# Attention on one core: the products with v in one burst of nine key tiles a unit instead of three bursts of three, with 18 buffers of probabilities instead of 9

## The reference, cut to what matters

```python
scores = jnp.einsum('bhqd,bhkd->bhqk', q, k) / math.sqrt(HEAD_DIM)
masked = jnp.where(causal[None, None], scores, NEG)
chunk_max = padded.reshape(b, N_HEADS, s, n_chunks, CHUNK).max(axis=-1)
_, topk_idx = jax.lax.top_k(chunk_max, k_top)
...
final = jnp.where(allowed, scores, NEG)
attn = jax.nn.softmax(final, axis=-1)
out = jnp.einsum('bhqk,bhkd->bhqd', attn, v)
```

## Time and profile before

| | |
|---|---|
| time, median of 3 runs | 1484.44 us (1482.44 to 1486.02) |
| profiled execution: its time | 1490.9 us |
| profiled execution: its span | 1489.0 us |
| PE busy over the span | 1292.4 us (87%) |
| DVE busy | 1021.5 us (69%) |
| ACT busy | 873.5 us (59%) |
| L1305, exponents (ACT) | 576 of 612 ns |
| L1225, masked scores (PE) | 576 of 396 ns |
| L1244, products with v (PE) | 4608 records of 276 ns |

### The profile page before, as it was taken

The page is one execution under the profiler, slowest core; times in us unless marked ns, Lnnn a source line. Parts: engine busy times, 40 slices in busy tenths (PEclk is TensorE's granted clock), DMA queues, the critical chain, the costliest instruction groups (busy, mean ns, idle before and its releaser), DMA issues. The chain is left out here.

```text
span 1489.0 us, 34856 instructions
## 1 busy us (share of the span) xinstructions
PE 1292.4 (87%) x10654; PEld 706.9 (47%) x10750; DVE 1021.5 (69%) x3215; ACT 873.5 (59%) x1605; POOL 449.2 (30%) x1388
## 2 busy tenths in 40 slices
PE   8957999999996996699899898998988989986995
PEld 3423444444443553355455455554555545543653
DVE  5875656556563599588788787887878878852563
ACT  2524625444250565377787687786767867872553
POOL 3530000000002233233334333433434334331665
PEclk9975999999998998599999999999999999998997
DMA  9310000000000266301110011110111101002221
GB/s 325 158 43 0 1 1 0 0 0 0 0 1 3 71 164 164 131 26 40 41 39 32 11 39 41 39 39 8 36 41 39 39 7 39 9 9 57 57 79 43
DMA packets 65131, 69.73 MB, mean 47 GB/s; under 512 B 35214, under 2 KB 53774, under 8 KB 64300
## 3 DMA queue, kind: packets, MB, share of 16 engines
q1 hardware_dynamic: 64940, 67.38, 14.2%
HBM read 36.96 MB, written 19.92 MB: 38 GB/s over the span
## 5 line engine op out<-in xcount | busy, mean ns | idle before, releaser
L1305 ACT ACTIVATE arena<-bank 128x512 f32<-128x512 f32 x576 | 340.2, 612 | 171.4 <-PE bank L1225 97.8
L1365 DVE TENSOR_REDUCE arena<-bank 128x32 f32<-128x512 f32 x528 | 343.8, 683 | 104.3 <-PE bank L1211 65.7
L1211 PE MATMUL bank<-arena 96*128 96x512 bf16 (+3 forms) x832 | 235.7, 333 | 25.2 <-issue 20.6
L1225 PE MATMUL bank<-arena 123*128 123x512 bf16 x576 | 222.8, 396 | 14.9 <-ACT arena L1305 12.3
L1244 PE MATMUL bank<-arena 128*32 128x128 f32 x4608 | 176.3, 276 | 12.6 <-ACT arena L1305 12.4
L579 PE MATMUL bank<-arena 128*128 128x512 f16 (+1 forms) x704 | 173.3, 390 | 0.0
L1475 POOL TENSOR_SCALAR arena<-arena 128x128 bf16<-128x128 bf16 x384 | 142.6, 371 | 47.5 <-DVE arena L1425 25.5
L1244 PEld LDWEIGHTS bank<-arena 128*32 128x32 f32 x4608 | 124.8, 109 | 43.2 <-ACT arena L1305 23.8
L1463 POOL TENSOR_TENSOR arena<-arena 128x4 f32<-128x4 f32 x128 | 25.4, 199 | 373.0 <-DVEq L1400 343.1
L205 POOL TENSOR_TENSOR arena<-arena 128x1 f32<-128x1 f32 x32 | 7.5, 234 | 388.8 <-DVE arena L201 388.4
L591 PE MATMUL bank<-arena 128*128 128x512 f16 (+1 forms) x528 | 118.4, 386 | 3.1 <-ACT arena L651 3.1
(11 more groups left out here) (183 smaller groups left out, 2252.6 us busy)
## 6 DMA issues: line engine op xcount, KB each, us to landing
arena<-qk_rows SPq DMA_DIRECT2D x16, 960.0 KB, 4.8
qk_rows<-arena SPq DMA_DIRECT2D x16, 768.0 KB, 4.1
arena<-arena SPq DMA_DIRECT2D x32, 256.0 KB, 2.9
arena<-in_x SPq DMA_DIRECT2D x4, 1024.0 KB, 12.4
out<-arena SPq DMA_DIRECT2D x16, 256.0 KB, 2.1
qk_rows<-arena SPq DMA_DIRECT2D x16, 192.0 KB, 4.6
arena<-in_down_qT SPq DMA_DIRECT2D x1, 2816.0 KB, 25.6
arena<-in_up_qT SPq DMA_DIRECT2D x1, 2752.0 KB, 19.4
```

The source lines that it names most:

```text
L1211: last = pe.matmul(bank[:, at:at + k1 - k0], query_aug[st.slot][0:ROWS, h * P:(h + 1) * P], key_aug[st.p][0:ROWS, k0:k1], start=True, stop ...
L1225: last = pe.matmul(bank[:, :], key_aug[st.p][0:KROWS, j * P:(j + 1) * P], query_aug[st.slot][0:KROWS, f * N:(f + 1) * N], start=True, stop ...
L1305: act.activation(probs[u % PROBS], back_bank[u % 2][:, :], ACT.Exp, scale=float(HD) ** -0.5).then_inc(probs_ready, 1)
L1365: dve.tensor_reduce(out=cm[:, number * per:(number + 1) * per], in_=score_bank[bank_of_score(front, number)][:, :].rearrange("p (c d) -> p ...
```

## The change

All tiles of a unit are weighed in one burst. With `BURST = 9` the schedule has one step "burst" a unit, at 0.985; the two at 0.448 and 0.733 are gone. The number of matmuls is the same. There are 18 buffers of probabilities, the nine new ones from the space that other small tiles of the stage are taken from. The exponent's wait on `summed` now points 18 tiles back instead of 9. ACT, DVE and POOL have the same work in the same order.

```diff
-    BURST, PROBS = 3, 9
+    EARLY_PROBS = 9
+    BURST, PROBS = 9, 18
...
-    probs = [take(N) for _ in range(PROBS)]
+    probs = [(take if n < EARLY_PROBS else spare)(N) for n in range(PROBS)]
```

## The result

The changed kernel takes 1507.03 us (median of 4 runs, 1505.23 to 1510.89), the kernel before 1485.23 beside it: a ratio of 1.0152, 95% interval 1.0126 to 1.0178, or 19 to 26 us more. The forecast was 1513 and 1497 to 1533. The profiled execution spans 1504.9 us. That is only 15.9 more than the one before, because what stands ahead of the first exponent took 7.0 us less in it (and what follows the last one 2.1 more); from the first exponent to the last, attention takes 736.2 us instead of 715.4, 20.8 more.

A forecast was written before the change was run, and what follows sets the result against it. A loop through ACT and PE bounds attention, no engine being full. Four units pay 5.28 us and get back 3.50, so 1.78 more; 16 times that, 28.5 us, gives 1513 us, range 1497 to 1533.

The forecast's parts named there:

- The loop through both engines: Attention units: first masked tile, nine exponents, last burst, next first masked tile set the time; chance 0.79 for 1497 to 1533.
- the 96.5 us: Attention: claimed as all the time ACT waits for masked tiles.
- Paid, 0.22 us a tile: Burst behind a unit's last exponent: six tiles more cost 1.32 us a unit, 5.28 us in four.
- Given back, kind by kind: Second halves of the four unit kinds: last exponent comes earlier by 0.88, 0.71, 0.85 and 1.06, together 3.50 us.
- Counted at nothing: DVE's wait for scores, copies of the sums behind the burst, and the new buffers: claimed to add nothing.
- sixteen times that: All of attention: 1.78 us more in four units, taken 16 times, gives 28.5 us, all units counted alike.
- for scores that arrive late: Upper side of the range: 20 us allowed above the forecast, up to 1533.
- the bound of 15 us: Second halves of units: if every idle moment of ACT there went, the change would still cost 15 us.
- PE is the bound: Rival, PE's bursts: each has a fixed 0.22 us, 128 go, 28 us faster, near 1456; chance 0.10.
- Nothing comes back: Rival, second halves: freed time lost as scores wait for DVE, 1569, half lost 1541; chance 0.07 for more than 1533.

The follow-up runs named there:

- e3: Kernel before with 18 buffers and two bursts a unit, three tiles at 0.448 and six at the end: 1482.18 us, ratio 0.9972 to before.
- e2: Kernel before with 18 buffers and two bursts a unit, six tiles at 0.733 and three at the end: 1517.72 us, ratio 1.0215 to before.
- e4: Changed kernel with its one end burst weighing only three of a unit's nine tiles, the rest left out: 1423.95 us, ratio 0.9582 to before.
- e1: Kernel before with only the 18 buffers added, still three bursts of three a unit: 1485.78 us, ratio 1.0007 to before.
- v3: Kernel before with 18 buffers, each unit's third burst of three and the copies of the sums moved into the next unit: 1441.54 us, ratio 0.9705.
- v9: Changed kernel with its burst of nine moved into the next unit at 0.11, copies of the sums behind it: 1477.79 us, ratio 0.9945 to before.

## Why the prediction was right

- *The bound.* The loop through both engines was the right reading: e3, before, after and e2, with 2, 3, 1 and 2 bursts a unit, fall in the order that the loop forecast (1484, 1485, 1513, 1521; measured changes of -4, 0, 22 and 32 us), not in that of the number of bursts, and two of them are told apart by 36 us with the same number. One row was misread on the way: the 96.5 us are not "in all" what ACT waits for masked tiles, which is 166.8; nothing in the sum uses it.
- *Paid, 0.22 us a tile.* The burst of 72 records holds PE for 2.11 us (1062.85 to 1064.96) against 0.80: 1.31, forecast 1.32. e4 has the term alone: 5.08 for four units, forecast 5.28.
- *Given back, kind by kind.* The units 7+0, 4+3, 6+1 and 5+2 grew by 0.60, 0.43, 0.47 and 0.24 us (11.57, 11.33, 11.00 and 11.08 against 10.97, 10.90, 10.53 and 10.84). Forecast were 1.32 less 0.71, 0.88, 0.85 and 1.06, which is 0.61, 0.44, 0.47 and 0.26. In 4+3 the last masked tile starts 1.44 behind the seventh exponent (1061.57 - 1060.13), before 2.33 (1056.12 - 1053.79): 0.89 earlier, forecast 0.88.
- *Counted at nothing.* First halves unchanged, DVE's busy time unchanged, and e1 shows the buffers at nothing. DVE does wait longer for scores, 130.3 us in attention instead of 108.5, but the idle time that it had took this up: the units grew by no more than the terms of the sum.
- *The size of the whole.* Forecast were 28.5 us, measured 22 (19 to 26). The term that was off is "sixteen times that". The units agree; what the sum did not have is what lies between them. PE jumps back six times in attention's loop over the groups, with a wait each time (20.6 us in all before, 18.8 after). In the profiled executions the units at these six places were 29.6 us longer than their kind before and 24.7 after (28.6 in e1, 26.5 in e2). The waits are 1.8 of these 4.9 us; the rest goes with PE's granted clock behind them. These are the 6 us from PE's first matmul behind a jump, one jump before and one after (columns as above):

```profile
831.55:837.55 6.00, 6.00 (x23) 3.00 (x23) 3.97 (x8) 3.95 (x9) 0.00 (x0) 0.50 0.03 5
1019.98:1025.98 6.00, 5.43 (x38) 3.06 (x40) 4.91 (x11) 5.06 (x11) 0.00 (x0) 1.00 0.01 4
```

In such stretches the clock was 0.56, 0.50, 0.73, 0.72, 0.50 and 0.50 before (0.50 is the 1.2 GHz level), with 5.1, 5.1, 4.1, 4.3, 5.4 and 5.6 us lost; after it was 0.72, 0.50, 0.72, 1.00, 0.72 and 0.50, with 3.8, 5.3, 3.8, 3.1, 3.8 and 4.9. So the jumps behind which the clock is slow for longer are the ones that cost more; why it was slow for less in the kernel after is open. The rest of the difference is within what runs of one kernel scatter.
- *The range.* Its upper side, 20 us "for scores that arrive late", was worked out from no row, and its lower end of 1497 is some 2 us under the bound of 15 us (1484.4 + 15 = 1499). Neither was needed.
- *The rivals.* "PE is the bound" fell with e2. The rule of the Trainium skill that stood behind it (TensorEngine Tiling (Array Packing), Key Properties: a change of tiling mode drains the array) agrees with a pause that the rows of before show, 0.22 us a burst; that this pause is that drain was not tried. In 4+3 the pause is part of the 0.88 us by which the last masked tile starts sooner, so it counts once, in what comes back; if it counted by the number of bursts, e2 would have been faster than before. "Nothing comes back" fell with e4, which was forecast at 1485 by it and took 1423.95.

## What to carry to other kernels

When no engine is full but the time repeats like a clock, look for the loop that goes through several engines and ask of each piece of work whether it lies inside the loop beside something or between the last step of one engine and the first of the next. Gathering work into long bursts saves the engine that does it a little, and costs the burst's length if it is put where the other engine has nothing left; the same burst half a unit later, under the other engine's full stretch, costs little as long as that engine has work for its whole length: the burst of three cost 0.23 us of its 0.88 there (v3), the burst of nine left ACT idle for 1.57 of its 2.10 (v9, unit 4+3). Give extra buffers the job of making that later place possible, not of making the burst longer.

## What the runs showed of the hardware that was not expected

Where the first burst of a unit follows the turning of the mask, the trace shows no pause between them. The transposes write partitions 96 to 122 of their bank, the burst's first six records (heads 0 to 2) partitions 0 to 95 of theirs. In the kernel before (PE, the first burst of a unit 7+0) these six records stand among the last three of eight transposes:

```profile
1040.77 0.45 PE L1198 MATMUL bank<-arena 128*27 128x128 bf16 x5
1041.01 0.31 PE L1244 MATMUL bank<-arena 128*32 128x128 f32 x3
1041.06 0.28 PE L1198 MATMUL bank<-arena 128*27 128x128 bf16 x2
1041.15 0.29 PE L1244 MATMUL bank<-arena 128*32 128x128 f32 x3
1041.17 0.22 PE L1198 MATMUL bank<-arena 128*27 128x128 bf16 x1
1041.23 0.82 PE L1244 MATMUL bank<-arena 128*32 128x128 f32 x18
```

The pause of 0.08 us ahead and 0.14 us behind a burst was seen next to matmuls over all 128 columns.

At the jump back of the loop PE waits in every kernel, 16 to 25 us in six places. In the kernel before and after, those waits are (total us, times, longest us):

```profile
PE bank L1211 <- issue: 20.6, 6, 3.6
```

```profile
PE bank L1212 <- issue: 18.8, 6, 3.3
```

PE waits about 3 us at each. With the slower clock that is granted behind most of them, 3.1 to 5.6 us are lost. That is the next 25 to 30 us to look at in this stage.

In e4 the six units at the jump were only 20.4 us longer than their kind, 9 less than before, which is the part of its gain that the units don't explain. PE's six waits there are 18.0 us in all, and behind two of them the clock stayed at 1.00; these two lost 2.3 us each, the others 3.6 to 4.8. Why the clock stayed there was not tried.
